# Splitting the second block's attention weights on ScalarE: two exponentials per strip, the second in place in PSUM

## The reference, cut to what matters

```python
def _L1_conv_ref(x, ...):
    xf = x.reshape(b_, c_, n)                      # 128 channels, 1024 pixels
    q = _conv1x1_bn(xf, q_w, ...)                  # 16 rows
    k = _conv1x1_bn(xf, k_w, ...)                  # 16 rows
    v = _conv1x1_bn(xf, v_w, ...)                  # 128 rows
    attn = softmax(einsum('bci,bcj->bij', q, k), axis=-1)      # 1024 x 1024
    out = einsum('bcj,bij->bci', v, attn)
    return gamma[0] * out + x
```

## Time and profile before

| | us |
|---|---|
| median of 3 runs | 405.02 |
| lowest and highest run | 403.21, 407.89 |
| profiled execution, first to last instruction (span) | 403.1 |
| PE busy | 341.7 (85%) |
| DVE busy | 260.5 (65%) |
| ACT busy | 198.8 (49%) |
| POOL busy | 27.3 (7%) |

### The profile page before, as it was taken

How to read it: one execution, slowest core, us unless ns; L and a number is a source line. 1 busy time by engine, 2 the same in 40 slices (tenths; PEclk the granted TensorE clock), 3 DMA queues, 4 the chain that set the end, 5 groups by cost and what they waited for, 6 DMA issues and landing times. The chain is left out here.

```text
span 403.1 us, 4422 instructions
## 1 busy us (share of the span) xinstructions
PE 341.7 (85%) x1408; PEld 237.8 (59%) x1408; DVE 260.5 (65%) x425; ACT 198.8 (49%) x351; POOL 27.3 (7%) x35
## 2 busy tenths in 40 slices
PE   3999777999998989999999899996599657597296
PEld 2853644785666847656775686672468356565162
DVE  1576777897598669876977797569397431301605
ACT  2445585646686646385685555667452433211000
POOL 3211100000021000002010000061001000100000
PEclk9999899999999699999998999996697957777579
DMA  7500000000000000000000000059600000000005
GB/s 247 188 0 2 0 1 0 2 0 0 2 0 3 0 0 2 0 0 2 0 0 0 0 0 0 0 192 411 230 2 0 0 2 0 0 0 2 1 0 208
DMA packets 5778, 15.08 MB, mean 37 GB/s; under 512 B 1294, under 2 KB 1998, under 8 KB 5762
## 3 DMA queue, kind: packets, MB, share of 16 engines
q0 software_dynamic: 2304, 8.39, 5.9%
q1 hardware_dynamic: 3458, 6.49, 4.6%
HBM read 12.78 MB, written 2.10 MB: 37 GB/s over the span
## 5 line engine op out<-in xcount | busy, mean ns | idle before, releaser
L373 PE MATMUL acc<-e,v0n 128*128 128x512 f32 x128 | 58.9, 595 | 0.9 <-DVE v0n L828 0.8
L659 ACT ACTIVATE e<-tile,nmax 128x1024 f32<-128x1024 f32 x22 | 24.5, 1115 | 38.8 <-DVE nmax L821 29.1
L860 DVE TENSOR_TENSOR e1l<-e,e1h 128x1024 fp32r<-128x1024 f32 x32 | 39.5, 1248 | 0.7
L373 PEld LDWEIGHTS acc<-e,v0n 128*128 128x128 f32 x128 | 23.5, 189 | 24.6 <-issue 20.1
L698 ACT ACTIVATE e<-tile 128x1024 f32<-128x1024 f32 x25 | 25.7, 1027 | 20.7 <-DVE e1l L860 13.9
L821 DVE TENSOR_REDUCE nmax<-tile 128x1 f32<-128x1024 f32 x22 | 26.9, 1222 | 11.0 <-PE tile L373 10.5
L864 DVE TENSOR_REDUCE nmax<-tile 128x1 f32<-128x1024 f32 x27 | 32.1, 1216 | 2.4 <-PE tile L373 2.4
L373 PE MATMUL tile<-ks,qs 96*128 96x512 f32 (+2 forms) x82 | 27.2, 426 | 6.1 <-ACT tile L688 4.2
L688 ACT ACTIVATE tile<-tile,nmax 128x1024 f32<-128x1024 f32 x27 | 29.4, 1087 | 3.0 <-DVE nmax L864 2.8
L857 DVE CAST e1h<-e 128x1024 fp32r<-128x1024 f32 x32 | 21.7, 687 | 3.5 <-ACT e L698 3.4
L373 PEld LDWEIGHTS tile<-ks,qs 96*128 96x128 f32 x82 | 15.3, 209 | 14.6 <-issue 8.1
(11 more groups left out here) (202 smaller groups left out, 678.6 us busy)
## 6 DMA issues: line engine op xcount, KB each, us to landing
cas_h<-in_cas_h_in POOLq DMA_DIRECT2D x8, 512.0 KB, 9.6
cas_l<-in_cas_l_in POOLq DMA_DIRECT2D x8, 512.0 KB, 10.4
xin<-in_x SPq DMA_DIRECT2D x4, 512.0 KB, 4.7
out<-xin SPq DMA_DIRECT2D x3, 512.0 KB, 2.6
zexp<-in_region_in SPq DMA_DIRECT2D x2, 360.0 KB, 4.7
out<-xin SPq DMA_DIRECT2D x2, 256.0 KB, 2.4
bins<-in_bins_in SPq DMA_DIRECT2D x1, 372.0 KB, 5.1
x3s<-in_near_in SPq DMA_DIRECT2D x1, 288.0 KB, 5.6
```

The source lines that it names most:

```text
L373: return nc.tensor.matmul(o, lhsT, rhs, start=start, stop=stop, skip_group_check=skip)
L659: nc.scalar.activation(e0[:, i % RING0, :], t[:, :], ACT.Exp, bias=nmax0[:, i:i + 1], accum_out=sum0[:, i:i + 1]).then_inc(s["e0_ready"], 1)
L860: vec.tensor_tensor(e1l[:, i % RING, :], e1[:, i % STAGE, :], e1h[:, i % RING, :].bitcast(F32), ALU.subtract).then_inc(s["e1l_ready"], 1)
```

## The change

ACT takes the exponential of each `scoreT` strip twice: first from the PSUM tile into `e1h`, with rounding to float32r, then in place in the PSUM tile in full. DVE's cast is gone; its subtraction reads the tile in PSUM and `e1h`. The SBUF ring `e1` is gone, and the tile of a `scoreT` strip is free for PE only when the subtraction is done.

```diff
-STAGE = 2
 RING = 3
@@ STEADY
-... scoreT:0 scoreT:1 e1h:0 gram:4 scoreT:2 e1l:0 e1h:1 e1l:1 mix:2 scoreT:3 gram:5 e1h:2 attend:0
-attend:1 scoreT:4 e1h:3 scoreT:5 attend:2 e1l:2 e1l:3 attend:3 scoreT:6 e1h:4 e1l:4 e1h:5 e1l:5 e1h:6
-attend:4 e1l:6 e1h:7 e1l:7 scoreT:7 attend:5 gram:6 attend:6 attend:7 x2:0 ...
+... scoreT:0 scoreT:1 gram:4 scoreT:2 e1l:0 e1l:1 mix:2 scoreT:3 gram:5 attend:0
+attend:1 scoreT:4 scoreT:5 attend:2 e1l:2 e1l:3 attend:3 scoreT:6 e1l:4 e1l:5
+attend:4 e1l:6 e1l:7 scoreT:7 attend:5 gram:6 attend:6 attend:7 x2:0 ...
@@ L12_ALL: the same, with e1h:0 to e1h:7 taken out of the list and nothing else moved
@@ LAST_READER
-               "scoreT": ("e1_ready", "b", CH, lambda i: i + 1), ...
+               "scoreT": ("e1l_ready", "b", CH, lambda i: i + 1), ...
@@ ACT
                     elif name == "scoreT":
                         t = take(step)
-                        wait_past(act, s["e1l_ready"], b * CH + max(i - STAGE + 1, 0))
-                        nc.scalar.activation(e1[:, i % STAGE, :], t[:, :], ACT.Exp).then_inc(s["e1_ready"], 1)
+                        wait_past(act, s["e1_used"], b * CH + max(i - RING + 1, 0))
+                        nc.scalar.activation(e1h[:, i % RING, :], t[:, :], ACT.Exp).then_inc(s["e1h_ready"], 1)
+                        nc.scalar.activation(t[:, :], t[:, :], ACT.Exp).then_inc(s["e1_ready"], 1)
@@ DVE
-                    elif name == "e1h":
-                        dve.wait_ge(s["e1_ready"], b * CH + i + 1)
-                        wait_past(dve, s["e1_used"], b * CH + max(i - RING + 1, 0))
-                        vec.tensor_copy(e1h[:, i % RING, :], e1[:, i % STAGE, :]).then_inc(s["e1h_ready"], 1)
                     elif name == "e1l":
-                        dve.wait_ge(s["e1h_ready"], b * CH + i + 1)
-                        vec.tensor_tensor(e1l[:, i % RING, :], e1[:, i % STAGE, :],
-                                          e1h[:, i % RING, :].bitcast(F32), ALU.subtract).then_inc(s["e1l_ready"], 1)
+                        t = slots[ph.slot(("scoreT", i))]
+                        dve.wait_ge(s["e1_ready"], b * CH + i + 1)
+                        wait_past(dve, s["e1_used"], b * CH + max(i - RING + 1, 0))
+                        vec.tensor_tensor(e1l[:, i % RING, :], t[:, :], e1h[:, i % RING, :].bitcast(F32),
+                                          ALU.subtract).then_inc(s["e1l_ready"], 1)
```

More of the change, by code:

```diff
@@ L79 @@
     "qkproj:0 qkproj:1 qklow:0 join elu:0 qklow:1 elu:1 zelu:0 zelu:1 score:0 score:1 score:2 score:3 "
[4 rows of a table removed]
-    "xkeep chanT")
[4 rows of a table added]
 END = steps(
@@ L98 @@
                "shift1": ("qs2_ready", "b", 2, lambda i: 1), "shift2": ("qs2_ready", "b", 2, lambda i: 2),
-               "scoreT": ("e1_ready", "b", CH, lambda i: i + 1), "asproj": ("full_ready", "b", 4, lambda i: i + 3),
+               "scoreT": ("e1l_ready", "b", CH, lambda i: i + 1), "asproj": ("full_ready", "b", 4, lambda i: i + 3),
                "x2T": ("x2T_ready", "b", 1, lambda i: 1),
@@ L278, in conv_seq @@
         with ExitStack() as l1_only:
-            e1 = l1_only.enter_context(nc.sbuf_tensor("e1", [P, STAGE, N], F32))
             e1h = l1_only.enter_context(nc.sbuf_tensor("e1h", [P, RING, N], F32R))
@@ L287, in conv_seq @@
         coef2 = sb("coef2", [P, CH, 2, BM], F32R)
-        sb("l1_rest", [P, (STAGE + 2 * RING) * N - 7 * CH * BM])
+        sb("l1_rest", [P, 2 * RING * N - 7 * CH * BM])
         x2 = sb("x2", [P, N])
@@ L852, in _ @@
                                           ).then_inc(s["v1_ready"], 1)
-                    elif name == "e1h":
+                    elif name == "e1l":
+                        t = slots[ph.slot(("scoreT", i))]
                         dve.wait_ge(s["e1_ready"], b * CH + i + 1)
                         wait_past(dve, s["e1_used"], b * CH + max(i - RING + 1, 0))
-                        vec.tensor_copy(e1h[:, i % RING, :], e1[:, i % STAGE, :]).then_inc(s["e1h_ready"], 1)
-                    elif name == "e1l":
-                        dve.wait_ge(s["e1h_ready"], b * CH + i + 1)
-                        vec.tensor_tensor(e1l[:, i % RING, :], e1[:, i % STAGE, :],
-                                          e1h[:, i % RING, :].bitcast(F32), ALU.subtract).then_inc(s["e1l_ready"], 1)
+                        vec.tensor_tensor(e1l[:, i % RING, :], t[:, :], e1h[:, i % RING, :].bitcast(F32),
+                                          ALU.subtract).then_inc(s["e1l_ready"], 1)
                     elif name == "score":
```

## The result

The changed kernel takes 446.98 us (median of 4 runs, 446.40 to 448.74), the kernel before 405.51 in the runs beside it: ratio 1.1024, 95% interval 1.0972 to 1.1077. The forecast was 435, its range 426 to 446. The sign and most of the size were right. The kernel is 12 us slower than forecast, and 1 us past the end of the range.

A forecast was written before the change was run, and what follows sets the result against it. PE was taken to bound the steady turns. Waits for held scoreT tiles, 24.9 us in three steady turns plus 5.5 in the last, add 30.4 to the 405.0 median: 435 us, range 426 to 446 with the clock's case.

The forecast's parts named there:

- What bounds the kernel: Steady turns, scoreT:0 to attend:7: PE's matmuls set the length, so work taken from DVE shortens nothing by itself.
- Prices of the added and changed operations: Per strip on ACT and DVE: each exponential about 1.03 us, subtraction from PSUM 1.22 us.
- the 65 ns: Skill's extra DVE overhead on PSUM against SBUF; with ACT's smaller overhead there, under 1 us in all.
- Steps 1 to 4: Steady turn: PE idles 2.7 us before scoreT:2, 2.7 before attend:0, 2.2 before scoreT:4, then 0.36 twice; sum 8.3.
- the walk: Second steady turn and last turn traced in each engine's fixed order: 8.3 us more per steady turn, 5.5 in the last.
- the caveat: Skill's rule: PSUM helps ACT only if TensorE doesn't need most of it; its cost is the steady turns' waits.
- the quicker destination: Skill's rule that ACT writes faster to PSUM; would make the sum some 0.03 us a pair shorter.
- The last turn: Last turn: PE held before attend:0, scoreT:5 and scoreT:7 until the subtraction is done; 5.5 us longer.
- the first rival: Steady turns: granted clock also falls as PE idles, about +2.5 us each, +10, so 445; chance 0.12.
- The sum: Waits of three steady turns, 24.9 us, plus last turn, 5.5: 30.4 us in total, without slower matmuls.
- the hold is harmless: scoreT slots: next fills come later than the subtraction, so only ACT's load counts; 405 us, chance 0.06.
- DVE's relief wins: Last turn: slots not wanted early and PE's idle came from the cast; -1.8 us, 403, chance 0.04.

The follow-up runs named there:

- two_exps_sbuf: Changed kernel, but the second exponential goes to the SBUF ring e1, so the tile needn't wait for the subtraction; 413.3 us, ratio 1.0198 to the kernel before.
- fed: Changed kernel plus zero-adding matmuls ahead of the three steps per turn, last turn included, at which PE waited; 431.1 us, ratio 1.0635 to the kernel before.
- sub_first: Changed kernel with DVE's subtractions e1l:0 and e1l:2 ahead of the maxima of gram:4 and gram:5 in the steady list; 432.5 us.
- sbuf_hold: Changed kernel with the second exponential into SBUF ring e1, the PSUM tile still held until the subtraction is done; 447.8 us.
- hold_only: Kernel before, one exponential, with each cast directly ahead of its subtraction and the tile held until that subtraction is done; 435.6 us, ratio 1.0716.
- base_fed: Kernel before plus zero-adding matmuls between each xproj's pieces: eight of 256 columns, 402.3 us, or four of 512, 403.4 us.

## Why the prediction was right, and where not

**What bounds the kernel: right.** PE sets the steady stretches. DVE's 20 us bought nothing: `two_exps_sbuf` has them too and is 2% slower than the kernel before.

**Prices of the added and changed operations: right.** 1023 ns for the exponential in place (1.03 taken), 1223 for the subtraction from PSUM (1.22 taken, from four rows). The subtraction from SBUF in `two_exps_sbuf` takes 1227 ns. So the 65 ns that the Trainium skill, "Perfetto Trace Analysis", section "Optimizing Scalar/DVE Operations", adds for DVE on PSUM do not show.

**Steps 1 to 4, the waits: right,** to 0.1 us a stretch where the clock is kept up (`fed`: 8.2 against 8.3). The walk's own check on the 8.3 was loose: it set its end of attend:7, 176.5, against 168.18, and against mix:3's start at 168.41 its shift is 8.1. The two agree this closely in part by luck, since the walk's PE steps are 0.2 us short between scoreT:2 and attend:0 (4.0 for the 4.2 of the earlier trace rows) and the wait it puts there is as much too long. In the changed kernel itself the waits are shorter, 2.45, 2.45 and 1.98 us in place of 2.7, 2.7 and 2.2; the starts agree nonetheless (scoreT:2 5.01 us after scoreT:0, 5.09 by the walk), since the walk let a step end when the next could have begun and the trace counts to the modelled end of its last matmul. That DVE's order lengthens the first two waits held as well (`sub_first`). The tile's place made no difference (`sbuf_hold`), its being needed by PE did. This bears out the caveat that the prediction took from the Trainium skill, "ScalarE: Activation LUTs", section "Step-by-step: what each stage is for"; that PSUM is the quicker destination does not show (1023 ns in place, 1024 into SBUF).

**The last turn: low by 2.** 5.5 us forecast, 7.5 measured, 4.4 with PE fed (at 0.94, a higher clock than the 0.86 of the kernel before). The waits were right here too: 5.8 us on `e1l`, against 0.2 in the kernel before, at the three steps that the walk named.

```profile
330.86 1.19 PE L369 MATMUL acc<-e1h,v1h 128*128 128x512 f32 x2 [2.77 <-DVE e1l L854]
...
337.98 0.70 PE L369 MATMUL tile<-qs,ks 96*128 96x512 f32 x2 [1.51 <-DVE e1l L854]
...
343.52 0.70 PE L369 MATMUL tile<-qs,ks 96*128 96x512 f32 x2 [1.56 <-DVE e1l L854]
```

The other 1.9 us is PE busy for longer (24.61 for 22.73 us), with the clock at 0.73 in place of 0.86.

**The step that failed is the weighing of the first rival, "the clock falls as well".** The sum put this term at nothing, and it is what happened. Between the profiles of `fed` and the changed kernel it measures 3.0, 2.8, 2.9 and 3.1 us in the four stretches, 11.7 together, about the 12 by which the forecast was short. The rival's price, 2.5 us a turn, was near, its time, 445, was 2 us off, and it got a chance of 0.12. I argued against it from the earlier trace rows: PE busy 2.16 of 4 us with the clock at 1.00, "less busy than my walk makes any 4 us but one or two". That reading of the walk was wrong. Its waits of 2.7, 2.7 and 2.2 us leave PE busy 1.3, 1.3 and 1.8 of the 4 us around them, so each steady turn has three such places, nine in all. The row itself is a mean over scattered idling, in which the longest wait is 1.43 us. It is also one case; the changed kernel has waits of 2.45 us with a fall behind them and, at 171.7, without. Four turns with three waits each should have made some falls the likely case, and the likeliest time 445, not 435. The runs `fed` and `sub_first` show that the falls hang on the idling: with work in the waits there was none in the steady turns, and with shorter waits there were fewer.

The Trainium skill, "TensorE: Matmul & The Clock Gate", section "A second HAM failure mode: psum-queue depth-cycling", tells of a kernel that cycles PSUM banks, idles briefly between groups of matmuls, and whose clock keeps dropping and recovering for it. The trace of the changed kernel agrees (0.61 and 0.59 behind two waits of 2.45 and 1.98 us). Weighed against the sum, it would have spoken for the first rival.

**The other rivals:** "the hold is harmless" and "DVE's relief wins" both needed slots that are not wanted at once; PE waits at three slots in every steady turn. And even with the hold gone neither would have come true: `two_exps_sbuf`, in which PE waits for ACT's second exponential instead, is still 2% slower than the kernel before.

## What to carry to other kernels

Before an operation is moved so that it reads a rotating PSUM tile, write out who gives each tile back and when the next fill of it is wanted; here two more steps in that time cost 8 us in a stretch of 21, though every engine but PE had idle time. In a kernel in which PE is the bound, price every forecast wait twice: its length, and the slow matmuls that may follow it. Giving a buffer back sooner (one subtraction ahead of one maximum) gained 15 us here, and reordering PE's own work around the wait on top of it gained nothing more.

## What the hardware showed that was not expected

- PE never idle and yet near half clock: in the kernel before, 132 to 139 us is 7.00 of 7.00 us busy at clock 0.53, from the second half of xproj's 16-column matmuls on. Eight 256-column matmuls of zeros between them kept it at 1.00 there, although PE is then busy only 6.11 of 7 us. The stationary operand of the added matmuls is all zeros, so a product of zeros keeps the clock up as well.
- The same wait is followed by a fall or not: in `hold_only` one of 3.17 us is followed by 1.00 and the next, of 3.18, by 0.63.
- Added PE work made two kernels faster: the changed one from 447.0 to 431.1 us with 116 more matmuls in the trace (1524 against 1408), the one before by 0.65% with 32.
- The part behind attend:7, in which only the two `base_fed` kernels differ from the kernel before, takes 84.9 to 88.6 us in the profiles, at a clock of 0.78 to 0.74. That is 3.7 us; the kernel before's first four runs spread over 4.7 (403.2 to 407.9).
